# Biases of keys and values written into the PSUM banks ahead of the products, for 22 of 32 token pairs

## The reference

```python
q = heads(x @ Wq + bq);  k = heads(x @ Wk + bk);  v = heads(x @ Wv + bv)
q = elu(q) + 1;          k = elu(k) + 1
k = k / sqrt(sum(k * k, axis=-1) + 1e-6)
attn = (q @ k^T) @ v                        # no softmax
y1 = layernorm(x + attn @ Wo + bo) * gamma + beta
x1 = layernorm(x + y1)
out = layernorm(x1 + fp4(silu(fp4(x1) @ fp4(w_gate)^T) * (fp4(x1) @ fp4(w_up)^T)) @ fp4(w_down)^T)
```

## Time and profile before

| | us |
|---|---|
| median of 3 runs | 709.93 (709.53 to 710.73) |
| the profiled execution | 708.07 |
| its span | 706.3 |

### The profile page before, as it was taken

One profiled execution on the slowest core, in us unless ns is written; L12 is line 12 of the kernel. 1 busy time (PEld: TensorE's weight loads), 2 busy tenths in 40 slices (PEclk: granted clock), 3 DMA queues, 4 the chain that ended last, 5 costly groups with the idle time before them and its releaser, 6 DMA issues.

```text
span 706.3 us, 14225 instructions
## 1 busy us (share of the span) xinstructions
PE 687.0 (97%) x4370; PEld 603.7 (85%) x4370; DVE 595.3 (84%) x1452; ACT 484.9 (69%) x943; POOL 607.2 (86%) x947
## 2 busy tenths in 40 slices
PE   8999999999988999999999999999999999999995
PEld 6887788788767799999999999999999999999995
DVE  6788878876887888898898898898898998998774
ACT  5766767666666767767767767767767767767664
POOL 3989888988877999988988988988988988989766
PEclk9999999999998999999999999999999999999999
DMA  9533443344322011111111111111111111100001
GB/s 278 173 135 135 135 139 133 121 145 155 106 98 83 31 61 45 61 45 47 61 59 46 60 46 45 58 64 46 61 46 46 59 61 46 60 17 16 16 32 45
DMA packets 22271, 55.05 MB, mean 78 GB/s; under 512 B 2546, under 2 KB 5556, under 8 KB 22196
## 3 DMA queue, kind: packets, MB, share of 16 engines
q1 hardware_dynamic: 21776, 54.01, 22.6%
q10 hardware_dynamic: 420, 0.13, 0.1%
HBM read 28.90 MB, written 25.17 MB: 77 GB/s over the span
## 4 chain that ended last, share of the span: by engine, by line
PE 90%; DVE 3%; issue 2%; POOL 2%; ACT 2%; DMA 1%; SPq 0%; POOLq 0%; DVEq 0%; ACTq 0%
PE banks L377 23%; PE banks L379 22%; PE banks L378 22%; PE banks L514 8%; PE banks L487 7%; PE banks L415 2%; PE banks L388 2%; PE banks L528 1%; PE banks L527 1%; PE banks L401 1%; PE banks L444 1%; DMA arena<-in_L_attn_x_dram 1%; PE banks L452 1%; POOL arena L1118 1%; DVE arena L795 0%
## 5 line engine op out<-in xcount | busy, mean ns | idle before, releaser
L377 PE MATMUL banks<-wgu_hi,actT_lo 128*128 128x512 f32 (+1 forms) x384 | 150.1, 391 | 1.5 <-DVE actT_lo L916 1.5
L378 PE MATMUL banks<-wgu_lo,actT_hi 128*128 128x512 f32 (+1 forms) x384 | 144.2, 376 | 0.0
L379 PE MATMUL banks<-wgu_hi,actT_hi 128*128 128x512 f32 (+1 forms) x384 | 143.6, 374 | 0.0
L683 ACT ACTIVATE arena<-banks 128x512 f32<-128x512 f32 x64 | 38.3, 599 | 114.0 <-PE banks L379 113.9
L1118 POOL TENSOR_TENSOR arena<-arena 128x960 f32<-128x960 f16 (+2 forms) x68 | 115.1, 1693 | 0.0
L1094 POOL TENSOR_TENSOR arena<-arena 128x704 f32<-128x704 f32 x64 | 89.1, 1393 | 20.6 <-DVE arena L903 18.6
L377 PE MATMUL banks<-wd_hi,actT_lo 128*128 128x256 f32 x320 | 100.1, 313 | 0.0
L916 DVE TENSOR_TENSOR actT_lo<-banks,actT_hi 128x512 fp32r<-128x512 f32 (+1 forms) x132 | 85.5, 674 | 16.4 <-ACT actT_hi L669 15.8
L379 PE MATMUL banks<-wd_hi,actT_hi 128*128 128x256 f32 x320 | 90.3, 282 | 0.0
L378 PE MATMUL banks<-wd_lo,actT_hi 128*128 128x256 f32 x320 | 90.2, 282 | 0.0
L377 PEld LDWEIGHTS banks<-wgu_hi,actT_lo 128*128 128x128 f32 x384 | 72.7, 189 | 10.7 <-DVE actT_lo L916 2.1
(11 more groups left out here) (126 smaller groups left out, 1925.6 us busy)
## 6 DMA issues: line engine op xcount, KB each, us to landing
xs<-x_plus_scratch SPq DMA_DIRECT2D x32, 512.0 KB, 3.3
x_plus_scratch<-xs SPq DMA_DIRECT2D x24, 512.0 KB, 2.9
arena<-in_L_attn_x_dram SPq DMA_DIRECT2D x32, 256.0 KB, 3.5
out_dram<-arena SPq DMA_DIRECT2D x32, 256.0 KB, 2.1
x_plus_scratch<-arena SPq DMA_DIRECT2D x8, 512.0 KB, 2.9
resid<-in_L_ffn_w_down_dram SPq DMA_DIRECT2D x1, 704.0 KB, 7.8
resid<-in_L_ffn_w_gate_dram SPq DMA_DIRECT2D x1, 640.0 KB, 8.2
resid<-in_L_ffn_w_up_dram SPq DMA_DIRECT2D x1, 640.0 KB, 9.7
```

Source lines behind the costliest of these rows:

```text
L377: nc.tensor.matmul(dst, sl, mh, start=(k == 0), stop=False, skip_group_check=shared)
L378: nc.tensor.matmul(dst, sh, ml, start=False, stop=False, skip_group_check=shared)
L379: last = nc.tensor.matmul(dst, sh, mh, start=False, stop=(ended and k == n - 1), skip_group_check=shared)
```

## The change

For pairs 2 to 23 (`filled`) ACT writes bk + 1 and bv, as a row of 512 values repeated for both banks, into the pair's two banks (128 x 1024 values). It does this one step ahead, in its step p-1, between `x_high` / `kv_out_copy` and `k_seeds`, after `k_features` and `v_bias` of pair p-2. The products of pair p wait for it and add to what is there: the first pass doesn't overwrite, and the two passes over `rows` are left out. `v_bias` is a copy there. bk is loaded once more, repeated on all partitions, and 1 is added on ACT before the first use. `bo_b` gets memory of its own, and bk's row takes the place next to bv's. Pairs 0, 1 and 24 to 31 are computed as before.

```diff
@@ sync, between the load of beta and load_x(2)
+            sp.dma_start(bkv[:, 0:D], bk.partition_broadcast(P)).then_inc(bk_in, 16)
@@ memory
+        bo_b = sb("bo_b", [P, D])
-        bv_b, bo_b = words(9587, D), words(9843, D)
+        bkv = words(9587, 2 * D)
+        bv_b = bkv[:, D:2 * D]
+        def filled(p):
+            return 2 <= p < MERGE
@@ tensor: split_product
-                    nc.tensor.matmul(dst, sl, mh, start=(k == 0), stop=False, skip_group_check=shared)
+                    nc.tensor.matmul(dst, sl, mh, start=(not begun and k == 0), stop=False, skip_group_check=shared)
@@ tensor: kv_project
+                if filled(p):
+                    pe.wait_ge(kv_bias, p - 1)
                 for jj in range(2):
...
-                    split_product(ps[:, bank, :], lambda k: (xT_hi[:, k, c], xT_lo[:, k, c]),
-                                  lambda k: (wkv_hi[:, k, :], wkv_lo[:, k, :]), KT, ended=False, shared=True)
-                    last = nc.tensor.matmul(ps[:, bank, 0:D], rows[:, D:], rows[:, 0:D], start=False, stop=True,
-                                            skip_group_check=True)
+                    last = split_product(ps[:, bank, :], lambda k: (xT_hi[:, k, c], xT_lo[:, k, c]),
+                                         lambda k: (wkv_hi[:, k, :], wkv_lo[:, k, :]), KT, begun=filled(p), ended=filled(p),
+                                         shared=True)
+                    if not filled(p):
+                        last = nc.tensor.matmul(ps[:, bank, 0:D], rows[:, D:], rows[:, 0:D], start=False, stop=True,
+                                                skip_group_check=True)
@@ scalar
+            def kv_biases(p):
+                if p == 2:
+                    act.wait_ge(bk_in, 16)
+                    act.wait_ge(bv_in, 16)
+                    nc.scalar.activation(bkv[:, 0:D], bkv[:, 0:D], ACT.Copy, bias=1.0).then_inc(bk_one, 1)
+                    act.wait_ge(bk_one, 1)
+                act.wait_ge(k_feat, p - 1)
+                act.wait_ge(v_s, p - 1)
+                b = kv_banks(p)
+                nc.scalar.activation(ps[:, b:b + 2, :], bkv[:, :].unsqueeze(1).broadcast_to([P, 2, 2 * D]),
+                                     ACT.Copy).then_inc(kv_bias, 1)
@@ scalar: first, ahead of k_seeds(p - 1)
                     kv_out_copy((p - 7) // PPB)
+                if filled(p + 1):
+                    kv_biases(p + 1)
@@ vector: v_bias
+                if filled(p):
+                    nc.vector.tensor_copy(vb[:, p % 3, :, :], ps[:, b:b + 2, D:2 * D]).then_inc(v_s, 1)
+                else:
                     nc.vector.tensor_tensor(vb[:, p % 3, :, :], ps[:, b:b + 2, D:2 * D],
                                             bv_b[:, :].unsqueeze(1).broadcast_to([P, 2, D]), ALU.add).then_inc(v_s, 1)
```

More of the change, by code:

```diff
@@ L173, in build @@
         G_BANK, U_BANK, GU_BANK, T_BANK, AT_BANK, DN_BANK = 6, 7, 0, 4, 2, (3, 1)
-        wk_in, wv_in, wq_in, wffn_in, rows_in, bv_in, bq_in, xb_in, late_in = (
-            sem(n) for n in ("wk_in", "wv_in", "wq_in", "wffn_in", "rows_in", "bv_in", "bq_in", "xb_in", "late_in"))
+        wk_in, wv_in, wq_in, wffn_in, rows_in, bv_in, bq_in, bk_in, xb_in, late_in = (
+            sem(n) for n in ("wk_in", "wv_in", "wq_in", "wffn_in", "rows_in", "bv_in", "bq_in", "bk_in", "xb_in", "late_in"))
         consts_set, small_set, cols_set, mask_s = sem("consts_set"), sem("small_set"), sem("cols_set"), sem("mask")
@@ L186, in build @@
         xT_ps, xT_hi_s, xT_lo_s = sem("xT_ps"), sem("xT_hi_done"), sem("xT_lo_done")
+        bk_one, kv_bias = sem("bk_one"), sem("kv_bias")
         kv_ps, k_exp, k_feat, v_s, k_sq, k_ssq, k_se, k_log, k_seed = (
@@ L372, in _, with split_product @@
         def _(pe):
-            def split_product(dst, stat, mov, n, ended=True, shared=False):
+            def split_product(dst, stat, mov, n, begun=False, ended=True, shared=False):
                 for k in range(n):
                     (sh, sl), (mh, ml) = stat(k), mov(k)
-                    nc.tensor.matmul(dst, sl, mh, start=(k == 0), stop=False, skip_group_check=shared)
+                    nc.tensor.matmul(dst, sl, mh, start=(not begun and k == 0), stop=False, skip_group_check=shared)
                     nc.tensor.matmul(dst, sh, ml, start=False, stop=False, skip_group_check=shared)
@@ L800, in v_bias @@
                 b = kv_banks(p)
-                nc.vector.tensor_tensor(vb[:, p % 3, :, :], ps[:, b:b + 2, D:2 * D],
-                                        bv_b[:, :].unsqueeze(1).broadcast_to([P, 2, D]), ALU.add).then_inc(v_s, 1)
+                if filled(p):
+                    nc.vector.tensor_copy(vb[:, p % 3, :, :], ps[:, b:b + 2, D:2 * D]).then_inc(v_s, 1)
+                else:
+                    nc.vector.tensor_tensor(vb[:, p % 3, :, :], ps[:, b:b + 2, D:2 * D],
+                                            bv_b[:, :].unsqueeze(1).broadcast_to([P, 2, D]), ALU.add).then_inc(v_s, 1)
             def k_sums(p):
```

## The result

| | us |
|---|---|
| before, runs on the same chip | 709.73, median of 6 (707.75 to 710.73) |
| after | 715.9, median of 6 (714.45 to 719.76) |
| ratio | 1.0106 [1.0084, 1.0128] |
| profiled execution of after (its span) | 714.45 (712.7), against 708.07 (706.3) |

The kernel is slower by about 1.1%: +6.2 us between the medians, +6.4 between the profiled executions, and +7.5 (6.0 to 9.1) by the ratio. 714.4 was forecast, with 4.5 of loss. The profiled execution is the fastest of the six; three of the others took 717.1 to 719.8, at a granted clock of 0.989 to 0.986 instead of 0.990, and have no timeline here.

The account below looks back on a forecast made before the run. PE was taken as the bound, with POOL, started by ACT's seeds, arriving together with it at turns of fresh chunks. Delays from the fill, less PE's arriving savings, summed to +4.5 us: 709.93 + 4.5 = 714.4 us, range 712 to 716.5.

Parts of the forecast that it names:

- The signs: Expected in the trace: k_newton about 3.3 us after its transposes, PE idle 1 us at turns, step 24 4.5 us later.
- PE's saving, 5.0 us: On PE, 44 passes over rows removed, 0.23 us a pair, 5.0 us in all: the most that can be won.
- F: Time one fill of 128 x 1024 takes in ACT's queue: estimated 0.97 us, ends 0.6 and 1.27.
- The copy instead of the sum: v_bias on DVE: taken at 0.68 us as before, no gain; otherwise the forecast could be 0.5 us lower.
- The row of bk: One more DMA row on 128 partitions, behind beta's: cost zero; if late, it delays ACT at pair 2.
- The turn of step 8: Turn of a fresh weight chunk: the seeds of step 7 come about F later, so +0.9 us.
- steps 2 to 6: PE could gain 5 x 0.23 us there, but ACT is behind from the start and doesn't catch up.
- Steps 9 to 18: Delays: +0.32 us at steps 9 and 13, -0.23 at 10 and 14, +0.97 at 11 and 15, +0.5 at 17.
- Step 19 to the turn of 22: Seeds F later; POOL works through until the chunk of step 21, and step 22 waits for it: +0.97 us.
- A: Rival: the fill lies in ACT's idle time, POOL doesn't hold the turns, the 5.0 us gain arrives: 704.9 us; chance 0.13.
- B: Rival: the two cancel, as the fill costs 0.6 us or only half the delays arise: 710.5 us; chance 0.16.
- C: Rival: the fill is dearer, F at 1.27 us, or ACT bounds every step: 716.5 us; chance 0.13.

Follow-up runs that it names:

- the best kernel: Changed kernel with the fill between k_exps and k_squares, weights turned one step later, queries projected ahead of kv_accumulate in steps 6, 10, 14 and on: 703.97 us.
- half fill: Changed kernel with only the keys' halves filled, 128 x 512, and the values' bias left out: 711.3 us, ratio 1.0029.
- the other two edits: Weights turned one step later and queries projected before kv_accumulate in steps 6, 10, 14 and on; on the changed kernel, fill ahead of the seeds: 709.48 us.
- the fill in the gap: Changed kernel with the fill moved on ACT from ahead of the seeds to between k_exps and k_squares: 709.12 us, ratio 0.9998.
- the kernel without bk's row: Kernel with passes and fill left out, biases of keys and values missing, and bk's row not loaded a second time: 708.64 us, ratio 0.9985.
- both edits of order: Turns one step later and queries' product before kv_accumulate: 708.61 us on before, 709.48 on the change, 703.97 with the fill between k_exps and k_squares.

## Why the prediction was right, and where it was off

Direction, mechanism and most of the size were right; the median of 715.9 lies near the upper end of the forecast's 712 to 716.5. The signs came as named: `k_newton` 3.28 us after its transposes, PE idle 1.36 and 1.38 us at the turns of steps 12 and 16 (where the view names x_low, though POOL's chunk is last at step 12), the same distance at step 24 and at the end. By its own steps:

- **PE's saving, 5.0 us.** Right at 0.23 a step (steps 9 to 23 in the table of delays), and right that hardly any would arrive. In the best kernel 3.6 of it does.
- **F, 0.97 us in ACT's queue.** Measured 0.95, lasting 1.03. The Trainium skill ("ScalarE: Activation LUTs", "Step-by-step: what each stage is for") has PSUM reached sooner than SBUF. The trace agrees with at most a small gain: 1.027 against the 1.06 worked out from rows with an SBUF target, 0.601 against 0.633 with 512 elements.
- **The copy instead of the sum, no gain.** 0.682 against 0.681. By the Trainium skill ("VectorE: DVE Perf Modes", "Why PSUM operands drop a tier") an fp32 operand in PSUM keeps VectorE in its 1x mode, and the trace agrees.
- **The row of bk, nothing.** The pair of kernels with and without its load shows no price, -0.9 and -1.1, good to about 1.
- **The turn of step 8, +0.9.** `k_newton` of step 7 comes at 49.83, before at 47.81: 2.02 later. Of this 0.95 is the fill. The rest, +1.13 between steps 6 and 7, is a term that the sum lacked:

```profile
43.57 0.69 PE L427 MATMUL banks<-arena 128*64 128x64 f32 x16 [1.30 <-DVE arena L855]
```

  `mask_heads` stands in DVE's queue behind `k_features`, k_sums and the rounding, and ends at 43.43 instead of 42.28. The 1.15 us are POOL's again: its x_biases end at 41.50 instead of 40.36, and with them the rounding, at 41.62 instead of 40.47. Before, PE used the result at 42.49, 0.2 us after it was there. I had priced "steps 2 to 6" as if PE only lost its gain there, and hadn't looked at how close the waits that read zero were.
- **Steps 9 to 18.** Turns of 12 and 16: forecast +0.97 each, measured from the start of step 11 to 13 +0.83 and from 15 to 17 +0.85, with the 0.23 that PE wins in steps 11 and 15 already in. Weights without a chunk (steps 9 and 13): +0.21 each instead of +0.32. Steps 10 and 14: -0.18 and -0.17 instead of -0.23. Step 17 with the turn of 18: +0.53, forecast 0.5. Together from step 9 to 19: +2.28, where the terms give 2.62.
- **Step 19 to the turn of 22, +0.97.** Measured +2.60 (4.24 to 6.84). `k_newton` of step 19 comes 5.19 later than before, which is 0.95 more than the step's start: right. Then POOL waits 0.73 us instead of 0.49 for DVE's rounding, and the turn at 146.27 is 5.45 late, 1.21 more than at step 19. The remaining 1.39 is TensorE's clock. The windows of after (busy of PE, PEld, DVE, ACT, POOL; then the granted clock):

```profile
144.00:145.50 1.50, 0.00 (x0) 0.00 (x0) 0.98 (x4) 1.47 (x3) 1.50 (x3) 1.00 0.07 27
145.50:147.00 1.50, 0.73 (x4) 0.72 (x4) 1.41 (x3) 0.00 (x1) 1.33 (x4) 0.68 0.98 330
147.00:148.50 1.50, 1.50 (x19) 1.10 (x17) 0.48 (x1) 1.11 (x3) 1.34 (x4) 0.50 0.51 167
...
150.00:151.50 1.50, 1.50 (x10) 1.25 (x9) 1.10 (x1) 0.00 (x0) 1.30 (x2) 1.00 0.00 0
```

  PE stands still for 3.26 us, what PE had saved in steps 19 to 21 included, and then runs at 0.50 (1.2 GHz) until it is back at 1.00. From the turn to the next step's transposes it takes 151.20 - 146.27 = 4.93 us, before 144.36 - 140.82 = 3.54, whence the 1.39, with PE busy throughout. I had priced a longer wait at its length alone.
- **The end.** +6.68 at step 24 and +6.4 at the end: after the merge nothing is won back, as forecast.

In sum: 4.5 + 1.1 (`mask_heads`) + 1.4 (clock) + 0.2 (POOL's wait) - 0.3 (steps 9 to 19) = 6.9, and the table has 6.84 at step 23. The 4.5 was short by the wait for `mask_heads` and by the clock, two terms that the sum had at nothing. This account is of one execution; the range's upper end, 716.5, came from F = 1.27, and that it was wide enough for the two is luck.

**The mechanism** holds at the turns, with one thing added. x_low arrives 0.3 us before POOL's chunk, but is itself held up by POOL, through the rounding. With POOL on time (fill behind the seeds) the wait there falls from 1.4 to 0.5 us, though k_exps is as late as in the change. I had read POOL as working without a pause but for the seeds; it also waits for the rounding, 0.20 us in step 11. What the prediction lacked are the hand-overs behind k_exps other than those of steps 9 and 13: in the kernel with POOL on time they, and the half clock that follows the one in step 6, bring the loss back to +6.7. What decides is that the fill stands ahead of the work that others wait for.

**The rivals.** A (704.9, the gain arrives) failed because the fill in ACT's queue delays what PE waits for. With the order changed in three places its number is reached (703.97), but 1.5 of those 5.1 us is the order's own. B (710.5, that is +0.6) would need F near 0.6, and its condition wasn't met. The half fill lasts 0.60 and gives +2.1 (1.2 to 2.9), so B's price was too low as well; its trace too has a wait for `mask_heads`, 0.56 us, and half clock after a stop of 2.56. C (716.5) came nearer to the median of 715.9 than the forecast did (714.4), but not by its mechanism: F isn't 1.27, and a plain step of ACT takes 5.26 us from fill to fill (24.00 to 29.27), even less than the 5.45 I worked out.

## What to carry to other kernels

Work moved from the bounding engine to one that is a third idle is paid for by its place in that engine's queue: ahead of the step's work it added 4.8 us (with the other two edits in) that it doesn't add in a slot where the engine waits anyway. Before such a move, list the hand-overs that read zero wait but have less slack than the new instruction lasts (here 0.1 and 0.2 us), on every way to them, those through a third engine included. And when a wait of the bounding engine grows, look for the clock after it.

## What the runs showed of the hardware that was not expected

**VectorE's rounding ends with GpSimd's instruction.** It lasts 0.19 us alone and up to 1.17 while POOL works, and 21 of 22 in two traces end 0.1 to 0.2 us after the POOL instruction beside them. That it waits for POOL is read from this; no run takes POOL's instruction away.

**Half clock after a stop.** The stop of PE ahead of step 22's turn was followed by a granted clock of 0.50 or little more in after (3.26 us), the half fill (2.56), the fill behind the seeds (2.39), the fill in the gap (2.29) and the kernel without bk's row (2.00). It wasn't in before (1.03), nor in two kernels with stops of 2.04 and 2.28 us, the one without passes and fill and the one with passes and fill. In step 6 stops of 2.72 us (fill behind the seeds) and 2.15 (turns later) were followed by it too. So the length of the stop alone doesn't decide. In the fill in the gap:

```profile
138.50:140.80 2.30, 0.08 (x1) 0.00 (x0) 2.30 (x6) 0.69 (x1) 2.30 (x4) 1.00 0.35 139
140.80:143.80 3.00, 2.93 (x23) 2.32 (x23) 0.77 (x2) 1.97 (x4) 2.67 (x6) 0.54 0.49 156
```

What decides it stays open; it is one reason why kernels that differ by 2 us at the start of step 22 end closer together or further apart.

**The first steps.** They start up to 3 us apart from trace to trace. In seven traces the first products stand 0.43 us apart for a while instead of 0.23, and step 2 begins 1.3 to 3.0 us later than in before: the fill in the gap, the fill behind the seeds, the change and the kernel before each with turns later, and the three kernels with both edits of order. The kernel before with turns later:

```profile
9.19 0.63 PE L378 MATMUL banks<-wkv_lo,actT_hi 128*128 128x512 f32 x1
9.61 0.63 PE L379 MATMUL banks<-wkv_hi,actT_hi 128*128 128x512 f32 x1
```

PE's program for these steps is that of before, where the two start at 8.72 and 8.96. The spacing is that of half clock; the column of the granted clock shows it in the best kernel alone (0.50 from 10 to 12 us). In other traces PE waits for x in step 3, 0.52 us in after and 1.96 without passes and fill. There is one trace of each kernel, so whether such a start belongs to the kernel or to the execution isn't known; bk's row isn't its cause, since two of the seven kernels don't load it twice.
